# Attention's edge tables built inside the spectral layer, and a mask step of one add and one maximum

## What is computed

```python
# spectral
agg = einsum('mn,bnd->bmd', U.T, x); h = relu(agg @ W1 + b1)
x = layernorm(x + einsum('nm,bmd->bnd', U, h @ W2 + b2))
# attention: 256 edges (src, dst), 4 heads of 32
e = einsum('behd,hd->beh', leaky_relu(Xq[:, src] + Xq[:, dst]), a) + log(adj[src, dst] + EPS)
m = segment_max(e, src); ex = exp(e - m[src]); attn = ex / segment_sum(ex, src)[src]
Y = segment_sum(attn * Xv[:, dst], src)
x = layernorm(x + Y @ W_out.T)
```

## Time and profile before

| | us |
|---|---|
| median of three runs | 4507.72 |
| lowest and highest | 4504.19, 4509.53 |
| profiled execution, own time | 4505.27 |
| profiled execution, span of its core | 4503.5 |
| last loop of the spectral layer | 4116.9 to 4171.9 |
| its norm | 4171.9 to 4187.2 |
| tables, sums, ones-matmul | 4187.2 to 4217.35 |
| gathering | 4217.35 to 4272.64 |
| mask stage | 4311.65 to 4421.06 |

### The profile page before, as it was taken

One profiled execution on the slowest core, in us unless ns is written; L12 is line 12 of the kernel. 1 busy time (PEld: TensorE's weight loads), 2 busy tenths in 40 slices (PEclk: granted clock), 3 DMA queues, 4 the chain that ended last, 5 costly groups with the idle time before them and its releaser, 6 DMA issues. The chain is left out here.

```text
span 4503.5 us, 78991 instructions
## 1 busy us (share of the span) xinstructions
PE 3280.2 (73%) x21600; PEld 2309.9 (51%) x21600; DVE 3563.7 (79%) x21360; ACT 1487.7 (33%) x5242; POOL 948.4 (21%) x3459
## 2 busy tenths in 40 slices
PE   4777776666666666677768877676983999979765
PEld 4676675556555665666654333232222566645532
DVE  6888888888887777777779999999997999322375
ACT  2333333333333333333324446444541111344104
POOL 2232232223333333322210024322330000000000
PEclk9955555555555555555559989898995999979856
DMA  2000000000000000000000000000000000000001
GB/s 77 2 2 2 2 2 2 2 2 2 1 2 1 1 1 1 1 1 1 1 1 1 1 1 1 1 1 1 1 1 0 1 1 1 1 1 1 0 0 38
DMA packets 14204, 17.76 MB, mean 4 GB/s; under 512 B 407, under 2 KB 10046, under 8 KB 13758
## 3 DMA queue, kind: packets, MB, share of 16 engines
q1 hardware_dynamic: 13758, 12.67, 1.0%
HBM read 8.47 MB, written 4.19 MB: 3 GB/s over the span
## 5 line engine op out<-in xcount | busy, mean ns | idle before, releaser
L623 PE MATMUL totals<-pp_sum,ones 128*128 128x2 f32 x768 | 225.4, 363 | 393.5 <-DVE pp_sum L429 392.2
L1144 DVE SCALAR_TENSOR_TENSOR lanes<-lanes,rows,poly 128x60 f32<-128x60 f32 x2048 | 481.3, 280 | 7.8
L1152 DVE SCALAR_TENSOR_TENSOR poly<-poly,off,lanes 128x60 f32<-128x60 f32 x2048 | 475.5, 268 | 0.0
L584 PEld LDWEIGHTS product<-x_parts,A_parts 128*128 128x128 bf16 x11136 | 425.9, 111 | 55.1 <-DVE A_parts L356 42.6
L584 PE MATMUL product<-x_parts,A_parts 128*128 128x3 bf16 x11136 | 400.8, 167 | 42.7 <-DVE A_parts L356 41.6
L623 PEld LDWEIGHTS totals<-pp_sum,ones 128*128 128x128 f32 x768 | 192.3, 311 | 426.2 <-DVE pp_sum L429 426.2
L543 POOL TENSOR_SCALAR x_scaled<-vwv,sc 128x4 f32<-128x4 f32 (+3 forms) x510 | 175.9, 345 | 1110.8 <-DVE corr_ae L414 518.1
L674 ACT ACTIVATE vwv<-v,sc 128x8 f32<-128x8 f32 (+3 forms) x510 | 152.3, 299 | 619.9 <-DVE sc L409 619.9
L914 PE MATMUL gate_ps<-h_sb,u 128*128 128x512 f32 (+1 forms) x504 | 322.3, 750 | 20.9 <-ACT gate L1032 20.9
L573 PE MATMUL coef<-x_on_pairs_sum,ones 128*128 128x4 f32 (+30 forms) x988 | 307.0, 404 | 40.6 <-ACT x_on_pairs_sum L687 23.6
L577 PE MATMUL row_e<-vwv,first 128*128 128x2 f32 (+28 forms) x924 | 282.5, 396 | 0.0
(11 more groups left out here) (514 smaller groups left out, 8428.1 us busy)
## 6 DMA issues: line engine op xcount, KB each, us to landing
out_dram<-x_sb SPq DMA_DIRECT2D x4, 1024.0 KB, 6.9
adj_sb<-adj_dram SPq DMA_DIRECT2D x1, 1024.0 KB, 5.7
alpha<-L_gnn_alpha_train_dram SPq DMA_DIRECT2D x1, 256.0 KB
w<-L_gnn_Wg_dram SPq DMA_DIRECT2D x2, 64.0 KB
w<-L_gnn_W_dram SPq DMA_DIRECT2D x2, 64.0 KB
edge_row<-L_gnn_src_dram SPq DMA_DIRECT2D x1, 128.0 KB
edge_row<-L_gnn_dst_dram SPq DMA_DIRECT2D x1, 128.0 KB
x_sb<-x_dram SPq DMA_DIRECT2D x4, 0.5 KB, 10.5
```

The costliest lines, as they stand in the source:

```text
L584: last = pe.matmul(product[:, r, 0:PARTS], parts[:, i, c, r * P:(r + 1) * P], x_parts[:, c, :], start=(c == c0 and i == 0), stop=(c == C - ...
L623: pe.matmul(totals[:, 0:2], k.ones[:], pp_sum[:], start=True, stop=True).then_inc(dot_ready, 1)
L1144: pair(dve.scalar_tensor_tensor(out=term[:, way, :], in0=flat, scalar=rows[:, way, row:row + 1], in1=poly[:, b, way, s + 1, :], op0=ALU.su ...
L1152: pair(dve.scalar_tensor_tensor(out=poly[:, b, way, s + 2, :], in0=poly[:, b, way, s, :], scalar=off2[:, way, row:row + 1], in1=term[:, wa ...
```

## The change

- `at_src`, `at_dst`, `at_any`, `src_t`, `same`, `a_cols` and `a_wide` are allocated before both layers, as is `weighed`, which takes the place of the first four rows of `gath`.
- GpSimd's memset of `a_cols` moves into the spectral Block.
- VectorE's table operations are put into steps 0 to 9 of the last spectral loop, behind that step's add. Those in a step are started together and waited for once. Only the sources are turned into columns (two multiplies, one reduce of 256 elements).
- TensorE does the two groups of sums behind the last loop, into `bank[0]` and `bank[1]`, 24 matmuls in all. VectorE copies and multiplies them behind its norm tiles, without waits between.
- Attention's TensorE program starts with the ones-matmul, VectorE's with its result.
- A step of the mask stage is one add and one reduce of 1024 elements each; scores and mask are both read repeatedly through a stride of zero.

Its core:

```diff
@@ spectral, TensorE, behind the last loop @@
+            pe.wait_ge(tables_ready, 1)
+            for e in range(EC):
+                for c in range(C):
+                    pe.matmul(bank[0][:, 0, e * E:(e + 1) * E], k.at_src[:, c, e * P:(e + 1) * P], k.at_src[:, c, :],
+                              start=(c == 0), stop=(c == C - 1))
+            for n in range(C):
+                for c in range(C):
+                    last = pe.matmul(bank[1][:, n // 2, (n % 2) * E:(n % 2 + 1) * E], k.adj_t[:, c, n * P:(n + 1) * P],
+                                     k.at_dst[:, c, :], start=(c == 0), stop=(c == C - 1))
+            last.then_inc(sums_ready, 1)
@@ spectral, VectorE, in the last loop behind its add @@
+                if j == 0:
+                    link(dve.tensor_copy(edge[:], k.edge_row[:]))
+                if 1 <= j <= C:
+                    link.start(dve.tensor_scalar(k.at_src[:, j - 1, :], edge[:, 0, :], k.node[:, j - 1:j], None, ALU.is_equal))
+                    link.start(dve.tensor_scalar(k.at_dst[:, j - 1, :], edge[:, 1, :], k.node[:, j - 1:j], None, ALU.is_equal))
+                if j == C:
+                    link.flush()
+                if j == C + 1:
+                    dve.tensor_tensor(k.at_any[:], k.at_src[:], k.at_dst[:], ALU.add).then_inc(tables_ready, 1)
+                if j == C + 2:
+                    for f in range(EC):
+                        link.start(dve.tensor_tensor(edge_junk[:, f, :], edge[:, 0, f * P:(f + 1) * P], k.ident[:], ALU.mult))
+                    link.flush()
+                    link(dve.tensor_reduce(edge_col[:], edge_junk[:], AX.X, ALU.add))
+                if j == C + 3:
+                    for f in range(EC):
+                        link.start(dve.tensor_scalar(k.src_t[:, f, :], k.iota[:], edge_col[:, f:f + 1], None, ALU.is_equal))
+                    link.flush()
+                if j == C + 4:
+                    dve.wait_ge(pool_done, 1)
+                    for h in range(HEADS):
+                        here = slice(h * DH, (h + 1) * DH)
+                        link.start(dve.tensor_copy(a_cols[here, h:h + 1], k.cols[here, 35:36]))
+                    link.flush()
+                if j == C + 5:
+                    for h in range(HEADS):
+                        link.start(dve.tensor_scalar(k.a_wide[:, h, :], k.ones[:], a_cols[:, h:h + 1], None, ALU.mult))
+                    link.flush()
             norm.dve_scale(dve)
             norm.dve_tiles(dve, DVE_TILES)
+            dve.wait_ge(sums_ready, 1)
+            link.start(dve.tensor_copy(k.same[:], bank[0][:, 0, :].rearrange("p (f e) -> p f e", e=E)))
+            for n in range(C):
+                link.start(dve.tensor_tensor(k.weighed[:, n, :], k.at_src[:, n, :],
+                                             bank[1][:, n // 2, (n % 2) * E:(n % 2 + 1) * E], ALU.mult))
+            link.flush()
@@ attention, TensorE @@
-                last = pe.matmul(area[:, 3, 0:E], k.ones[:], gath[:, c, :], start=(c == 0), stop=(c == C - 1))
+                last = pe.matmul(area[:, 3, 0:E], k.ones[:], k.weighed[:, c, :], start=(c == 0), stop=(c == C - 1))
@@ attention, VectorE, mask stage @@
-                    for half_ in range(2):
-                        for f in range(EC):
-                            link(dve.tensor_tensor(pair[:, half_, f, :], area[:, 6 + n % 2, half_ * E:(half_ + 1) * E],
-                                                   mask[:, f, :], ALU.add))
-                    for half_ in range(2):
-                        link(dve.tensor_reduce(top[:, :, b + half_, h], pair[:, half_, :, :], AX.X, ALU.max))
+                    scores = area[:, 6 + n % 2, :].rearrange("p (a e) -> p a e", e=E)
+                    link(dve.tensor_tensor(pair[:], scores.unsqueeze(2).broadcast_to([P, 2, EC, E]),
+                                           mask[:].unsqueeze(1).broadcast_to([P, 2, EC, E]), ALU.add))
+                    link(dve.tensor_reduce(top[:, :, b:b + 2, h].rearrange("p f a -> p a f"), pair[:], AX.X, ALU.max))
```

More of the change, by code:

```diff
@@ L1901, in _ @@
                 act.copy(k.h[:, b, :], bank[:, b % 4, :]).then_inc(used_act, 1)
+E = 256
+HEADS = 4
+EC = E // P
+DH = D // HEADS
 def spectral(nc, k):
@@ L1907, in spectral @@
         sb, ps, sem = allocators(nc, ctx)
+        edge = sb("edge", [P, 2, E])
+        edge_col = sb("edge_col", [P, EC])
+        edge_junk = sb("edge_junk", [P, EC, P])
+        a_cols = k.a_cols
+        pool_done = sem("a_cols_cleared")
+        tables_ready = sem("tables_ready")
+        sums_ready = sem("table_sums_ready")
+        table_link = sem("table_link")
         agg = sb("agg", [P, 2, N])
@@ L1956, in _ @@
                 last.then_inc(ready[3], 1)
+            pe.wait_ge(tables_ready, 1)
[8 more added lines that the diff above has]
+            last.then_inc(sums_ready, 1)
+        @block.gpsimd
+        def _(pool):
+            pool.memset(a_cols[:], 0.0).then_inc(pool_done, 1)
         @block.vector
         def _(dve):
+            link = Link(dve, table_link)
             dve.wait_ge(bias_sent, 1)
@@ L2051, in _ @@
             sp.wait_ge(stored, 16 * C)
-        @block.gpsimd
-        def _(pool):
-            pool.memset(a_cols[:], 0.0).then_inc(pool_done, 1)
         @block.tensor
@@ L2106, in _ @@
                     pe.matmul(area[:, 2, (e * B + b) * HEADS:(e * B + b + 1) * HEADS], lrelu[:, b, e * P:(e + 1) * P],
-                              a_cols[:], start=True, stop=True)
+                              k.a_cols[:], start=True, stop=True)
             for e in range(EC):
@@ L2130, in _ @@
                 for f in range(EC):
-                    last = pe.matmul(area[:, 0, e * 64:(e + 1) * 64], same[:, f, e * P:(e + 1) * P],
+                    last = pe.matmul(area[:, 0, e * 64:(e + 1) * 64], k.same[:, f, e * P:(e + 1) * P],
                                      score[:, f, :, :].rearrange("p b h -> p (b h)"), start=(f == 0), stop=(f == EC - 1))
@@ L2139, in _ @@
                     for f in range(EC):
-                        last = pe.matmul(area[:, i % 2, :], val[:, f, i, :], src_t[:, f, :], start=(f == 0), stop=(f == EC - 1))
+                        last = pe.matmul(area[:, i % 2, :], val[:, f, i, :], k.src_t[:, f, :], start=(f == 0), stop=(f == EC - 1))
                     mine(last)
@@ L2174, in mine @@
                 dve.drain().then_inc(dve_done, 1)
-            link(dve.tensor_copy(edge[:], k.edge_row[:]))
-            for i in range(2):
-                for f in range(EC):
[L2179 to L2198, removed]
             theirs()
@@ L2205, in _ @@
                 link(dve.tensor_reduce(log_col[:, f:f + 1], junk[:], AX.X, ALU.add))
-            link(dve.tensor_scalar(mask[:], same[:], 1.0, 1e30, ALU.subtract, ALU.mult))
+            link(dve.tensor_scalar(mask[:], k.same[:], 1.0, 1e30, ALU.subtract, ALU.mult))
             link(dve.tensor_tensor(mask[:], mask[:], log_row[:].unsqueeze(1).broadcast_to([P, EC, E]), ALU.add))
@@ L2321, in build @@
             back_transform(nc, k)
+        sb, _, _ = allocators(nc, ctx)
+        k.at_src = sb("at_src", [P, C, E])
+        k.at_dst = sb("at_dst", [P, C, E])
+        k.at_any = sb("at_any", [P, C, E])
+        k.weighed = sb("at_weighed", [P, C, E])
+        k.src_t = sb("src_t", [P, EC, N])
+        k.same = sb("same_src", [P, EC, E])
+        k.a_cols = sb("a_cols", [P, HEADS])
+        k.a_wide = sb("a_wide", [P, HEADS, P])
         spectral(nc, k)
```

34 lines of the change are left out of this document (4 added, 30 removed).

## The result

Four runs of the changed kernel took 4457.6 to 4461.25 us, a median of 4459.12, against 4507.73 for four of the kernel before (4504.19 to 4509.53). The ratio is 0.9893 with a 95% interval of 0.9881 to 0.9906: 48.6 us less. The prediction was 4460.1, within 4452 to 4468.

The account below looks back on a forecast made before the run. Limits differ by stage: a serial VectorE-TensorE stretch before the ones-matmul, VectorE in the mask stage. Savings of 23.3 + 24.3 = 47.6 us from 4505.27 give 4457.7, or 4460.1 as a median; range 4452 to 4468.

Parts of the forecast that it names:

- Part one: Tables and sums leave the serial stretch between norm and ones-matmul: 23.3 us saved, from 21.4 to 25.9.
- part two: Mask stage, 32 steps: one add and one reduce of 1024 each save 0.761 us a step, 24.3 us in all.
- The loop as cover: VectorE's table pieces, at most 1.26 us, fit its 2.75 us wait per step of the last spectral loop; cost nothing.
- The rival of delayed adds: Last spectral loop: table pieces delay its adds and TensorE; all 9.7 us exposed gives 4469.8 us; chance 0.03.
- TensorE's sums: 48 passes behind the last spectral loop take 10.4 us during the norm, leaving 4.9 us of cover.
- The tail of five operations: Copy and four multiplies behind VectorE's norm tiles, without waits: 2.2 us exposed, ends 2.1 and 2.5.
- The rule of the Trainium skill: Removing semaphores between VectorE operations gains nothing; the five behind the norm would take 2.5 us, the total gain 0.3 less.
- The block change: From VectorE's last operation in the spectral layer to attention's first matmul, the ones-matmul: 0.6 us.
- The clock: TensorE restarts at 1.2 GHz at the ones-matmul for 4.4 us; 0.6 us lost, ends 1.7 gained and 2 lost.
- The mask step: One mask-stage step takes 2.622 us: add 1.226, gap 0.036, reduce 1.220, and 0.14 to the next.
- TensorE being late: Mask stage: TensorE needs 2.2 us a step at low clock, below 2.62, so VectorE stays the limit.
- The slow rival: TensorE stays at 1.2 GHz in gathering, its 256 passes taking 110.6 us, not 55.3; 4518.9 us total; chance 0.03.

Follow-up runs that it names:

- burst: The changed kernel with all of VectorE's table pieces in step 0 of the last spectral loop; one run, 4461.99 us.
- narrow_unwaited: The changed kernel with mask steps of four 256-wide adds and two 512 reduces, each group started together and waited for once; 4467.88 us, ratio 0.9909.

## Why the prediction was right

By its own steps, from the profile after. Part one was to be 23.3 us and was 24.0 (24.2 by the earlier ones-matmul, less 0.2 of low clock); part two was to be 24.3 and was 24.5; the rest of attention gave back 0.3; together 48.2, beside 47.6. The parts are close one by one, so the sum isn't right by errors that cancel. The range was less well founded: its ends of 44.7 and 52 us of gain don't follow from the ends of the parts, which add up to some 42 and 51.5. The measured 48.6 lies inside both.

- The loop as cover: right. The pieces cost nothing there, and **burst** shows how much is too much. The rival of delayed adds had the price of all pieces, 9.7 us; even all at once cost only 2.1.
- TensorE's sums: 10.4 us at the high clock foreseen, 10.5 seen, with 4.8 us of cover (4.9).
- The tail of five operations: 2.2 foreseen, 1.92 seen, below the end of 2.1. The copy overlaps the last tile by 0.08 us too, which I had not counted. The rule of the Trainium skill that would have made it 2.5 failed.
- The block change: 0.6 foreseen, 0.54 seen. So the ones-matmul started 2.46 us after the last tile in place of 26.68: 24.2 earlier, not 23.9.
- The clock: this term was mis-sized. I took 4.4 us of low clock from three restarts and a loss of 0.6. The clock was low for 3.4 us, against 3.0 before; gathering began 3.49 after the start of the ones-matmul, against 3.30 before; the loss was 0.2. A similar amount was lost in another place, which the prediction didn't have: the eight passes of the first value sums took 6.42 us (from 4386.35), against 6.03 before (from 4430.62), since the clock rose after 5.5 us and not after 4.7; 0.1 of that 0.4 came back by the end. Both are the moment at which the clock rises, which I could only take from a spread.
- The mask step: 2.622 foreseen, 2.62 seen, with 1.225 for the add (1.226) and 1.222 for the reduce (1.220). Repeated operands, one of them from PSUM, cost nothing here. What the prediction did not ask is where the gain comes from. In the rows a waited-for add shows only 0.036 us of gap, but without the wait the next one started 0.333 us after it in place of 0.46, and **narrow_unwaited** shows that two thirds of the gain were to be had with the old shapes.
- TensorE being late: not at 2.62, as foreseen; the level of the clock did not matter to the step. My bound of 2.2 us for shorter steps was wrong in practice, since the clock rose with them.
- The slow rival, a clock that stays low in gathering, did not come in the changed kernel or in any experiment: behind the first sixteen passes the granted clock of that stage was 1.00 in each.

## What to carry to other kernels

When a chain of short VectorE operations has no dependence inside, start them together and wait once: it gave two thirds of what widening gave, and an operation that adds and keeps the maximum in one then gave more than the whole change to the mask step had. Put independent set-up work where the bounding engine never rests but another does, in pieces that fit one step's slack, and price the slack in steps that the waits allow, not in idle time. Move what runs cold (matmuls behind a pause) to the end of a dense stretch; hiding it there is worth its cold time.

## What was not expected of the hardware

VectorE operations of 256 f32 elements that are not waited for start 0.333 to 0.345 us apart though each is recorded at 0.42, and the write of a maximum (0.083 us in the records) ran beside the next operation. With the same two matmul passes in each step, TensorE's clock stayed at 2.4 GHz with steps of 1.82 us and below, went to and fro at 2.01 (mean 0.84), and fell to 1.2 GHz with steps of 2.62 and more; what the chip goes by was not tried.
